# Two passes of a transformer layer with experts: the key pass without TensorE transposes, and another order of work on ScalarE and VectorE in the expert pass

## Chip, cores and metric

The kernel runs on one core of a Trainium2 chip. The metric is the device time of one execution, in microseconds (us). Three runs of the kernel before took 6706.5, 6708.36 and 6711.54 us; the median is 6708.36 us.

## What is computed

`T` = 4096 tokens (4 batches of 1024) with `H` = 1024 features. In float32:

```python
def _layernorm(x): m, v = mean(x), var(x); return (x - m) / sqrt(v + 1e-5)
# cross attention, 16 heads of 64
q = layernorm(x) @ Wq.T + bq;  k = ctx @ Wk.T + bk;  v = ctx @ Wv.T + bv
probs = softmax(clip(where(mask, q @ k.T / 8, -1e4), -50, 50))
delta = (probs @ v) @ Wo.T + bo
x = x + layernorm(rs * delta) * gamma + beta
# experts: 64, each token goes to 8, I = 384
h = layernorm(x)
scores = softmax(h @ gate_weight.T); topk_w, topk_idx = top_k(scores, 8); topk_w /= sum(topk_w)
x = x + sum over the 8 of topk_w * ((silu(h @ w_gate[e]) * (h @ w_up[e])) @ w_down[e])
```

Every large product is made of three matrix products: each operand is split into a rounded part (`hi`, a cast on ScalarE) and the rest (`lo`, a subtraction on VectorE), and `hi*hi + hi*lo + lo*hi` is accumulated.

## The kernel before

The program is a chain of passes with a barrier between them: projections (keys K, values V, queries Q), attention, output with routing, and experts. All waits are written out by hand as semaphore waits, so each engine works through its own list in the order of the program text.

**Projections** (`projections_pass`). Three products K, V, Q, one after the other, each over 8 blocks of 512 tokens. A block has 8 rounds `g`, each of 24 matmuls of 512 columns (L420 to L422) into one of 4 PSUM banks; ScalarE and VectorE evacuate them (L293, L355), SyncE stores. Activations come by GpSimd's DMA queue into `a_raw` (L192) in 4 pieces, are split by `high` (L282) and `low` (L342) in rounds 0 to 3 of the block before, and are double-buffered as `a_hi`, `a_lo`. In the key pass VectorE also normalizes the 32 tiles of 128 tokens of `x` (`layernorm`, ending in `xn`, L373), one in every second round. TensorE turns each in 8 transposes of 128x128 (L431) into PSUM, ScalarE copies it out (`transposed`, L304), and SyncE stores it by features into the scratch `xnT` (L264), from which the query pass loads its activations.

**Experts** (`experts_pass`). Work goes by tiles of 128 routed tokens: 286 tiles in this run, for 64 experts, each with `n` tiles (read from `dir_sb`). `tile t` means, engine by engine in list order:

- TensorE: gate (24 matmuls of 384 columns, L1374 to L1376), up (24 more), then down of tile t-1 (18 matmuls of 512 columns, L1361 to L1363), then 3 transposes of `hidden` (L1381). At the first tile of an expert it waits piece by piece for that expert's split weights.
- ScalarE: `silu` of tile t (L1432), `xT_hi` of tile t+1 (L1408), `y` of tile t-1 from PSUM (L1414), `hT_hi` (L1438). In an expert's first tile the 8 pieces (128x768) of the next expert's gate and up weights are cast (L1402) between `xT_hi` and `y`, and the loads of the gate and up weights after those are issued at the end (`load_gate_up`, L1420; it waits until VectorE has done all 8 pieces). After the last tile of an expert come the 3 pieces of the next down weights (L1402), and then their next load (`load_down`, L1426; it waits for VectorE's 3 pieces). Then the numbers of the next expert are read from `dir_sb` into registers (L1250, L1251).
- VectorE: `hidden` = silu * weight * up (L1484), `xT_lo` of tile t+1 (L1471), the turn of the gathered tokens of tile t+2 in 32x32 blocks (L1477), in a first tile the 8 pieces of `gu_lo` (L1467), then `hT_lo` (L1491), and at the end of an expert the 3 pieces of `d_lo`.
- GpSimd: for tile t+3 it waits for the turn of t+2, makes the row numbers (L1321, 128x4 integers from the records in `rec_g`), waits for them, and issues 4 gathers (L1325); then it issues the scatter of `y` of tile t-1, which adds to `out` in DRAM (L1335).
- SyncE: small loads of records (L1262, L1277). The records of tile t+4 are loaded after the row numbers of tile t+3 are made.

`y` has one buffer, so the copy of `y` waits until the scatter before it has landed:

```python
def output(t, is_first=False):
    act.wait_ge(down_done, t + 2)
    if not is_first:
        act.wait_ge(added, 16 * (t + 1))
    nc.scalar.copy(y[:], y_ps[:]).then_inc(y_done, 1)
```

## Time and profile before

| what | value |
|---|---|
| median of 3 runs | 6708.36 us (6706.5 to 6711.54) |
| profiled execution, its time | 6714.65 us |
| its span | 6713.0 us |
| TensorE busy, matmuls / weight loads | 6472.6 us (96%) / 5731.1 us (85%) |
| VectorE, ScalarE, GpSimd busy | 3663.3, 2923.7, 2308.0 us |
| mean granted TensorE clock | 0.983 |
| first matmul of the expert pass | at 2852.5 us |
| GB/s moved over the span | 156 |

All times inside the kernel are those of the profiled execution, counted from its first instruction. A matmul's duration in the rows is longer than its share of TensorE's time, because matmuls overlap: in a run of them the distance between starts counts (0.23 us for 512 columns, 0.17 us for 384).

### The profile page before, as it was taken

The page shows a single profiled execution, that of the slowest core. Times are in us where ns is not written, and L with a number is a line of the kernel's source. Part 1 is how long each engine was busy: PE and PEld are TensorE (multiplying, and loading weights), DVE is VectorE, ACT ScalarE, POOL GpSimd, SP SyncE. Part 2 cuts the span into 40 slices and gives each one's busy share as a digit, 9 for nine tenths or more (in the row PEclk, how much of TensorE's full clock was granted, in tenths as well). Part 3 has the DMA queues.
Part 4 walks back from the last instruction along what each step waited for, and adds up shares of the span by engine and source line. Part 5 has one row for each costly group of instructions (what it writes and reads, how often), then busy time and mean ns, then how long its engine had stood idle before and what let it go on. Part 6 is the DMA issues. An engine that isn't in the chain of part 4 may idle for free.

```text
span 6713.0 us, 107844 instructions
## 1 busy us (share of the span) xinstructions
PE 6472.6 (96%) x32234; PEld 5731.1 (85%) x32235; DVE 3663.3 (55%) x4544; ACT 2923.7 (44%) x3606; POOL 2308.0 (34%) x2178
## 2 busy tenths in 40 slices
PE   9999999999999999699999999999999999999998
PEld 7888887887888788589989888899899999989987
DVE  4443324999999799744454454443533444444444
ACT  3321224888888655333343343332422333333333
POOL 1000000000000155544545454554444444545554
PEclk9999999999999999899999999999999999999999
DMA  8863555555555676456676676665655656666666
GB/s 258 232 196 143 155 146 144 127 128 127 128 132 130 174 173 171 110 152 160 163 212 162 164 188 160 163 164 111 186 111 111 139 137 164 146 155 164 161 158 149
DMA packets 873577, 1049.72 MB, mean 156 GB/s; under 512 B 440705, under 2 KB 670849, under 8 KB 873474
## 3 DMA queue, kind: packets, MB, share of 16 engines
q0 software_dynamic: 123984, 368.70, 24.0%
q1 hardware_dynamic: 593104, 382.50, 23.6%
q10 hardware_dynamic: 156386, 297.29, 13.2%
q8 instruction: 48, 0.79, 0.1%
q14 instruction: 55, 0.45, 0.0%
HBM read 725.85 MB, written 322.31 MB: 156 GB/s over the span
## 4 chain that ended last, share of the span: by engine, by line
PE 33%; DMA 8%; issue 6%; DVE 4%; POOL 3%; ACT 2%; ACTq 1%; SPq 0%; another core or an unknown queue 0%; POOLq 0%; DVEq 0%
DMA out<-moe_y,moe_rec_s 4%; PE moe_ps_gate L1374 4%; PE moe_ps_gate L1375 4%; PE moe_ps_gate L1376 4%; PE moe_ps_up L1376 4%; PE moe_ps_up L1374 4%; PE moe_ps_up L1375 4%; PE moe_ps_y L1363 3%; PE moe_ps_y L1362 3%; PE moe_ps_y L1361 3%; DMA moe_tokens<-h2st,moe_rows 3%; POOL moe_tokens L1325 2%; DVE moe_ps_turned L1477 1%; DVE moe_d_lo L1467 1%; DVE moe_gu_lo L1467 1%
## 5 line engine op out<-in xcount | busy, mean ns | idle before, releaser
L1325 POOL DMA_INDIRECT moe_tokens<-h2st,moe_rows x1156 | 1273.1, 1101 | 515.2 <-issue 265.7
L1374 PE MATMUL moe_ps_gate<-moe_gu_hi,moe_xT_hi 128*128 128x384 f32 x2288 | 811.3, 355 | 73.8 <-DVE moe_xT_lo L1471 53.9
L1414 ACT COPY moe_y<-moe_ps_y 128x1024 f32<-128x1024 f32 x287 | 291.2, 1015 | 1249.4 <-DMA out<-moe_y,moe_rec_s 1051.9
L1375 PE MATMUL moe_ps_gate<-moe_gu_lo,moe_xT_hi 128*128 128x384 f32 x2288 | 784.4, 343 | 0.0
L1376 PE MATMUL moe_ps_gate<-moe_gu_hi,moe_xT_lo 128*128 128x384 f32 x2288 | 783.4, 342 | 0.0
L1376 PE MATMUL moe_ps_up<-moe_gu_hi,moe_xT_lo 128*128 128x384 f32 x2288 | 764.3, 334 | 0.0
L1375 PE MATMUL moe_ps_up<-moe_gu_lo,moe_xT_hi 128*128 128x384 f32 x2288 | 764.2, 334 | 0.0
L1374 PE MATMUL moe_ps_up<-moe_gu_hi,moe_xT_hi 128*128 128x384 f32 x2288 | 764.2, 334 | 0.0
L1484 DVE SCALAR_TENSOR_TENSOR moe_hidden<-moe_silu,moe_rec_w,moe_ps_up 128x384 f32<-128x384 f32 x286 | 175.8, 615 | 1009.2 <-PE moe_ps_up L1376 694.4
L1361 PE MATMUL moe_ps_y<-moe_d_hi,moe_hT_hi 128*128 128x512 f32 x1722 | 673.5, 391 | 12.8 <-DVE moe_hT_lo L1491 10.3
L1363 PE MATMUL moe_ps_y<-moe_d_hi,moe_hT_lo 128*128 128x512 f32 x1722 | 677.1, 393 | 0.0
L1362 PE MATMUL moe_ps_y<-moe_d_lo,moe_hT_hi 128*128 128x512 f32 x1722 | 675.7, 392 | 0.0
L657 DVE TENSOR_TENSOR att_p_lo<-att_p,att_p_hi 128x1024 fp32r<-128x1024 f32 x512 | 626.5, 1224 | 58.9 <-ACT att_p_hi L626 53.2
L626 ACT CAST att_p_hi<-att_p 128x1024 fp32r<-128x1024 f32 x512 | 539.7, 1054 | 161.5 <-PE att_ps_o L597 158.0
L1321 POOL TENSOR_SCALAR moe_rows<-moe_rec_g,moe_group 128x4 int32<-128x4 int32 x289 | 156.6, 542 | 1245.5 <-DVE moe_ps_turned L1477 1190.1
L1491 DVE TENSOR_TENSOR moe_hT_lo<-moe_ps_hT,moe_hT_hi 128x384 fp32r<-128x384 f32 x286 | 158.8, 555 | 736.6 <-ACT moe_hT_hi L1438 646.3
L1335 POOL DMA_INDIRECT out<-moe_y,moe_rec_s x287 | 491.1, 1711 | 185.5 <-issue 177.1
L620 ACT ACTIVATE att_e<-att_ps_sc 128x1024 f32<-128x1024 f32 x512 | 522.5, 1021 | 10.3 <-PE att_ps_sc L583 10.3
L1477 DVE STREAM_TRANSPOSE moe_ps_turned<-moe_tokens 128x1024 f32<-128x1024 f32 x288 | 362.9, 1260 | 292.7 <-DMA moe_tokens<-h2st,moe_rows 272.7
L1374 PEld LDWEIGHTS moe_ps_gate<-moe_gu_hi,moe_xT_hi 128*128 128x128 f32 x2288 | 444.4, 194 | 86.1 <-issue 47.3
L1408 ACT CAST moe_xT_hi<-moe_ps_turned 128x1024 fp32r<-128x1024 f32 x287 | 290.8, 1013 | 511.1 <-PE moe_ps_up L1376 442.5
L1467 DVE TENSOR_TENSOR moe_gu_lo<-first_raw,moe_gu_hi 128x768 fp32r<-128x768 f32 x512 | 448.3, 943 | 0.4 <-ACT moe_gu_hi L1402 0.3
(202 smaller groups left out, 14047.6 us busy)
## 6 DMA issues: line engine op xcount, KB each, us to landing
first_raw<-in_w_gate ACTq DMA_DIRECT2D x63, 1536.0 KB, 7.7
first_raw<-in_w_up ACTq DMA_DIRECT2D x63, 1536.0 KB
moe_raw_d<-in_w_down ACTq DMA_DIRECT2D x63, 1536.0 KB
proj_a_raw<-in_ctxT POOLq DMA_DIRECT2D x64, 512.0 KB, 5.6
kst<-proj_o SPq DMA_DIRECT2D x256, 128.0 KB, 2.8
vst<-proj_o SPq DMA_DIRECT2D x64, 512.0 KB, 2.6
qst<-proj_o SPq DMA_DIRECT2D x256, 128.0 KB, 2.2
att_kt<-kst SPq DMA_DIRECT2D x64, 512.0 KB, 3.5
```

Of the source, the lines that this page charges most:

```text
L620: nc.scalar.activation(e32[:, u % 2], sc[:, u % 2], ACT.Exp, scale=1.0 / math.sqrt(HD)).then_inc(exp_done, 1)
L626: nc.scalar.copy(p_hi[:, u % 2], p32[:, u % 2]).then_inc(hi_done, 1)
L657: nc.vector.tensor_tensor(p_lo[:, u % 2], p32[:, u % 2], f32(p_hi[:, u % 2]), ALU.subtract).then_inc(lo_done, 1)
L1325: nc.gpsimd.indirect_dma_start(out=tokens[:, g * (H // G):(g + 1) * (H // G)], out_offset=None, in_=h2_quarters, in_offset=bass.IndirectOf ...
L1335: nc.gpsimd.indirect_dma_start(out=acc[:, :], out_offset=bass.IndirectOffsetOnAxis(ap=rec_s[:].bitcast(I32)[:, 0:1], axis=0), in_=y[:], in ...
L1361: nc.tensor.matmul(y_ps[:, cols], hT_hi[:, c], d_hi[:, b, c, cols], start=(c == 0), stop=False)
L1362: nc.tensor.matmul(y_ps[:, cols], hT_hi[:, c], d_lo[:, b, c, cols], start=False, stop=False)
L1363: last = nc.tensor.matmul(y_ps[:, cols], hT_lo[:, c], d_hi[:, b, c, cols], start=False, stop=(c == CI - 1))
L1374: nc.tensor.matmul(o[:, 0:I], xT_hi[:, c], gu_hi[:, b, k, c], start=(c == 0), stop=False)
L1375: nc.tensor.matmul(o[:, 0:I], xT_hi[:, c], gu_lo[:, b, k, c], start=False, stop=False)
L1376: last = nc.tensor.matmul(o[:, 0:I], xT_lo[:, c], gu_hi[:, b, k, c], start=False, stop=(c == C - 1))
L1467: nc.vector.tensor_tensor(low, raw, f32(high), ALU.subtract).then_inc(w_lo_done, 1)
```

## The change

Projections: the normalized tiles are stored as rows (`xnst`, tokens by features), with the columns of each row permuted by quarters in the write of `xn`. TensorE's 256 transposes, ScalarE's 32 copies and the PSUM tile are gone. In the query pass GpSimd's queue loads 512 token rows at a time (4 loads of 512 KB, each into 32 partitions) into `xg`, which takes the place of `xin` and `xn`, and VectorE turns them in 32x32 blocks, 4 turns of 128x1024 for each of the 8 query blocks, in rounds 0 to 3 of the block before, ahead of that round's evacuation. `high` and `low` read `a_raw` through a permuted view.

Experts: `silu` of tile t+1 is issued at the end of tile t, ahead of what follows a tile (weight pieces of the down product, register loads). Gate and up weights are split in 4 pieces of 128x1536 in place of 8 of 128x768, and they stand between other work. The three weight loads are issued at other places. Row numbers are made by VectorE. Scatter and gathers keep their order.

```diff
@@ projections, SyncE, then VectorE, then TensorE @@
+                            sp.dma_start(xnst[bass.ds(j * P, P), :], xn[:, jb]).then_inc(xn_stored[jb], 16)
...
+                def turn(p, t2, b, k):
+                    n = number(p, t2, b)
+                    dve.wait_ge(xg_in, 16 * (P // W) * (2 * t2 + b + 1))
+                    dve.wait_ge(a_lo_done, (n - 1) * PIECES + k + 1)
+                    columns_of_piece = slice(k * CP * W, (k + 1) * CP * W)
+                    nc.vector.transpose(a_raw[:, chunks(k)].rearrange("p c t -> p (c t)"), xg[:, :, columns_of_piece]).then_inc(turned_done, 1)
...
-                        dve.wait_ge(t_done, j - 1)
-                    nc.vector.tensor_scalar(xn[:, jb], xin[:, jb], mv[:, jb, 0:1], rstd[:, jb],
+                        dve.wait_ge(xn_stored[jb], 16 * (LN // 2 * (2 * t2 + b) + g // 4))
+                    nc.vector.tensor_scalar(by_quarter(xn[:, jb]), in_chunks(xin[:, jb]), mv[:, jb, 0:1], rstd[:, jb],
...
-                            for c in range(C):
-                                last = nc.tensor.transpose(tps[:, jb, c], xn[:, jb, c * P:(c + 1) * P], ident[:])
-                            last.then_inc(t_done, 1)
@@ experts, pieces and GpSimd @@
+        CHUNKS = C // 2
+        GU = 2 * C // CHUNKS
+        PIECES = GU + CI
...
                 def gather(t):
-                    pool.wait_ge(rec_g_in, 16 * G * (t + 1))
                     pool.wait_ge(turned_done, t)
                     pool.sem_inc(pool_passed, 1)
-                    nc.gpsimd.tensor_scalar(rows[:], rec_g[:].bitcast(I32)[:, :, 0], float(G), group[:], ALU.mult, ALU.add).then_inc(rows_done, 1)
                     pool.wait_ge(rows_done, t + 1)
@@ experts, end of TensorE's list @@
+                pe.wait_ge(hidden_done, last_tile + 2)
+                pe.sem_inc(gu_done, 1)
                 down(last_tile, (E - 1) % 2)
@@ experts, ScalarE @@
+                def load_gate_up(e, k):
+
+                    act.wait_ge(w_lo_done, PIECES * (e - 1) + (k + 1) * GU // 2)
...
+                def tile(t):
+                    tokens_high(t + 1)
+                    output(t - 1)
+                    turned_high(t)
+                    gated(t + 1)
+
+                def first_tile(t, e, b, more, is_first):
+                    tokens_high(t + 1)
+                    load_down(e)
+                    split(e, b, 0, 2)
+                    output(t - 1, is_first)
+                    split(e, b, 2, 3)
+                    turned_high(t)
+                    split(e, b, 3, GU)
+                    gated(t + 1)
                     if more:
-                        load_gate_up(e + 1)
+                        load_gate_up(e + 1, 0)
+                        load_gate_up(e + 1, 1)
...
                         split(e + 1, 1 - b, GU, PIECES)
-                        if has_second:
-                            load_down(e + 2)
@@ experts, VectorE @@
+                def token_rows(t):
+                    dve.wait_ge(rec_g_in, 16 * G * (t + 1))
+                    if not (isinstance(t, int) and t == 0):
+                        dve.wait_ge(gathered, 16 * G * t)
+                    nc.vector.tensor_scalar(rows[:], rec_g[:].bitcast(I32)[:, :, 0], float(G), group[:], ALU.mult, ALU.add).then_inc(rows_done, 1)
...
                     tokens_low(t + 1)
+                    if e is not None:
+                        split(e, b, 0, 1)
                     turn_tokens(t + 2)
+                    token_rows(t + 3)
                     if e is not None:
-                        split(e, b, 0, GU)
+                        split(e, b, 1, 2)
+                    if e is not None:
+                        split(e, b, 2, 3)
                     dve.wait_ge(hT_hi_done, t + 1)
                     nc.vector.tensor_tensor(hT_lo[:], hT_ps, f32(hT_hi[:]), ALU.subtract).then_inc(hT_lo_done, 1)
+                    if e is not None:
+                        split(e, b, 3, GU)
```

Here `gated(t)` is the `silu` of tile t with its two waits, `turned_high(t)` is `hT_hi`, and `tokens_high(t + 1)` is `xT_hi`.

## Rows read from the trace of the kernel before

**Rows 1.** The page, busy time of each engine over the span.
```profile
PE 6472.6 (96%) x32234; PEld 5731.1 (85%) x32235; DVE 3663.3 (55%) x4544; ACT 2923.7 (44%) x3606; POOL 2308.0 (34%) x2178
```
**Rows 2.** Groups by line, TensorE, first 1100 us: count | busy, mean ns | idle before.
```profile
L431 PE MATMUL proj_ps_tps<-proj_ident,proj_xn 128*128 128x128 f32 x256 | 33.1, 272 | 0.0
```
**Rows 3.** Timeline, TensorE, around one group of transposes: start us, us.
```profile
48.93 1.03 PE L431 MATMUL proj_ps_tps<-proj_ident,proj_xn 128*128 128x128 f32 x8
49.72 0.48 PE L420 MATMUL proj_ps_acc<-proj_a_hi,proj_w_hi 128*128 128x512 f32 x1
```
**Rows 4.** DMA issues by line: count, KB each, median us from issue to landing.
```profile
proj_a_raw<-xnT POOLq DMA_DIRECT2D x32, 512.0 KB, 4.4
```
**Rows 5.** TensorE's waits, 2853 us to the end: total us, times, longest.
```profile
PE moe_ps_hT L1381 <- DVE moe_hidden L1484: 61.4, 26, 3.2
PE moe_ps_gate L1374 <- DVE moe_xT_lo L1471: 53.9, 27, 37.8
```
**Rows 6.** View by tile of `hidden`: ns min/median/max, first and last start.
```profile
L1484 DVE SCALAR_TENSOR_TENSOR moe_hidden<-moe_silu,moe_rec_w,moe_ps_up x286: 612/615/618, 2865.7 to 6685.1; 128x384 f32<-128x384 f32 x143
```
**Rows 7.** Timeline, ScalarE, an expert's two tiles and the next expert's start.
```profile
4752.38 1.01 ACT L1408 CAST moe_xT_hi<-moe_ps_turned 128x1024 fp32r<-128x1024 f32 x1 [0.26 <-PE moe_ps_up L1376]
4753.29 5.98 ACT L1402 CAST moe_gu_hi<-first_raw 128x768 fp32r<-128x768 f32 x8
...
4765.50 0.49 ACT L1432 ACTIVATE moe_silu<-moe_ps_gate 128x384 f32<-128x384 f32 x1 [4.42 <-issue]
...
4775.48 1.02 ACT L1414 COPY moe_y<-moe_ps_y 128x1024 f32<-128x1024 f32 x1 [8.58 <-DMA out<-moe_y,moe_rec_s]
...
4776.76 2.95 ACT L1402 CAST moe_d_hi<-moe_raw_d 128x1024 fp32r<-128x1024 f32 x3
4781.51 0.39 ACTq L1426 DMA_DIRECT2D moe_raw_d<-in_w_down  x1
4783.65 0.49 ACT L1432 ACTIVATE moe_silu<-moe_ps_gate 128x384 f32<-128x384 f32 x1 [3.94 <-issue]
```
**Rows 8.** Timeline, VectorE, the same stretch and the tile before it.
```profile
4739.66 0.61 DVE L1484 SCALAR_TENSOR_TENSOR moe_hidden<-moe_silu,moe_rec_w,moe_ps_up 128x384 f32<-128x384 f32 x1 [6.72 <-PE moe_ps_up L1376]
...
4752.47 0.61 DVE L1484 SCALAR_TENSOR_TENSOR moe_hidden<-moe_silu,moe_rec_w,moe_ps_up 128x384 f32<-128x384 f32 x1 [2.83 <-PE moe_ps_up L1376]
...
4771.73 1.26 DVE L1477 STREAM_TRANSPOSE moe_ps_turned<-moe_tokens 128x1024 f32<-128x1024 f32 x1 [3.57 <-DMA moe_tokens<-h2st,moe_rows]
...
4784.43 0.61 DVE L1484 SCALAR_TENSOR_TENSOR moe_hidden<-moe_silu,moe_rec_w,moe_ps_up 128x384 f32<-128x384 f32 x1 [3.08 <-ACT moe_silu L1432]
```
**Rows 9.** Timeline, GpSimd, the same stretch.
```profile
4743.43 0.27 POOL L1321 TENSOR_SCALAR moe_rows<-moe_rec_g,moe_group 128x4 int32<-128x4 int32 x1 [4.98 <-DVE moe_ps_turned L1477]
...
4745.86 0.95 POOL L1325 DMA_INDIRECT moe_tokens<-h2st,moe_rows  x1 [0.30 <-issue]
...
4757.19 1.54 POOL L1321 TENSOR_SCALAR moe_rows<-moe_rec_g,moe_group 128x4 int32<-128x4 int32 x1 [4.80 <-DVE moe_ps_turned L1477]
4759.57 1.74 POOL L1325 DMA_INDIRECT moe_tokens<-h2st,moe_rows  x1 [0.84 <-POOL moe_rows L1321]
...
4766.26 1.63 POOL L1335 DMA_INDIRECT out<-moe_y,moe_rec_s  x1 [0.30 <-issue]
```
**Rows 10.** Timeline, TensorE, the transposes and the gate product after them.
```profile
4785.10 0.55 PE L1381 MATMUL moe_ps_hT<-moe_ident,moe_hidden 128*128 128x128 f32 x3 [2.95 <-DVE moe_hidden L1484]
...
4786.84 0.52 PE L1375 MATMUL moe_ps_gate<-moe_gu_lo,moe_xT_hi 128*128 128x384 f32 x1
4787.16 0.52 PE L1376 MATMUL moe_ps_gate<-moe_gu_hi,moe_xT_lo 128*128 128x384 f32 x1
```
**Rows 11.** Groups by line and shape, ScalarE and VectorE, 2853 us to the end.
```profile
L1402 ACT CAST moe_gu_hi<-first_raw 128x768 fp32r<-128x768 f32 x506 | 378.7, 838 | 12.3 <-DMA first_raw<-in_w_up 11.4 <-DMA first_raw<-in_w_gate 0.8
L1467 DVE TENSOR_TENSOR moe_gu_lo<-first_raw,moe_gu_hi 128x768 fp32r<-128x768 f32 x508 | 444.8, 943 | 0.4 <-ACT moe_gu_hi L1402 0.3
L1467 DVE TENSOR_TENSOR moe_d_lo<-moe_raw_d,moe_d_hi 128x1024 fp32r<-128x1024 f32 x192 | 223.8, 1221 | 34.6 <-ACT moe_d_hi L1402 25.2 <-issue 9.4
```

More of the change, by code:

```diff
@@ L146, in stores_before @@
         def stores_before(p, t2, b, g):
-            return 16 * (sum(STORES[i] * NB * G // 2 for i in range(p)) + STORES[p] * ((2 * t2 + b) * (G // 2) + g // 2))
+            return 16 * (sum(STORES[i] * NB * ROUNDS // 2 for i in range(p)) + STORES[p] * ((2 * t2 + b) * (ROUNDS // 2) + g // 2))
         def piece(p, half, k):
@@ L163, in norm_tile, with turned, split @@
             return LN * (2 * t2 + b) + g // 2 if g % 2 == 0 else None
-        def transposed_tile(p, t2, b, g):
-            if g % 2 == 0 or p == Q or p == V and not (is_first(t2, b) and g == 1) or p == K and is_first(t2, b) and g == 1:
-                return None
-            if p == V:
-                return LN * NB - 1
-            return LN * (2 * t2 + b) + (g - 3) // 2
-        def stored_tiles(p, t2, b, g):
-            return LN // 2 * (NB if p == V else 2 * t2 + b) + (g - 3) // 2 // 2
+        def turned(p, k):
+            raw = a_raw[:, chunks(k)]
+            if p < Q:
+                return raw
+            return raw.rearrange("p c t -> p (c t)").rearrange("p (g c b) -> p c g b", g=GROUPS, b=W)
+        def split(p, tile, b, k):
+            piece = tile[:, b, chunks(k)]
+            if p < Q:
+                return piece
+            return piece.rearrange("p c (g b) -> p c g b", b=W)
         def chunks(k):
@@ L188, in load @@
                     n, t = number(p, t2, b), 2 * t2 + b
+                    if p == Q:
+                        if not is_first(t2, b):
+                            pool.wait_ge(turned_done, PIECES * t)
+                        for k in range(P // W):
+                            part = xnst[bass.ds(t * HALF, HALF), k * (H * W // P):(k + 1) * (H * W // P)]
+                            pool.dma_start(xg[k * W:(k + 1) * W], part.rearrange("(g b) n -> b g n", b=W)).then_inc(xg_in, 16)
+                        return
                     for k in range(PIECES):
@@ L280, in high @@
                     n = number(p, t2, b)
[L281 to L282 removed]
+                    if p < Q:
+                        act.wait_ge(a_in[k], 16 * (n + 1))
+                    else:
+                        act.wait_ge(turned_done, (2 * t2 + b) * PIECES + k + 1)
+                    nc.scalar.copy(split(p, a_hi, b, k), turned(p, k)).then_inc(a_hi_done, 1)
                 def evacuate(p, t2, b, g):
[L285 removed]
+                    n, q = number(p, t2, b) * ROUNDS + g, g % 2
                     if not (p == K and is_first(t2, b) and g < 2):
@@ L298, in root @@
                     nc.scalar.activation(std[:, jb], mv[:, jb, 1:2], ACT.Sqrt, bias=eps[:]).then_inc(std_done, 1)
-                def transposed(j, jb, tiles_before):
-                    act.wait_ge(t_done, j + 1)
-                    if not (known(tiles_before) and tiles_before == 0):
-                        act.wait_ge(xT_stored[jb], 16 * tiles_before)
-                    nc.scalar.copy(xT[:, jb], tps[:, jb]).then_inc(xT_done, 1)
                 for k in range(PIECES):
@@ L316, in body @@
                         weights_high(p, 1, 1)
-                    for g in range(G):
+                    for g in range(ROUNDS):
                         evacuate(p, t2, b, g)
@@ L386, in body @@
                         weights_low(p, 1, 1)
-                    for g in range(G):
+                    for g in range(ROUNDS):
+                        if after and after[0] == Q and g < PIECES:
+                            turn(*after, g)
                         evacuate(p, t2, b, g)
@@ L1371, in tile @@
                         for c in range(C):
-                            if e is not None and c % 2 == 0:
-                                pe.wait_ge(w_lo_done, PIECES * e + k * (C // 2) + c // 2 + 1)
+                            if e is not None and c % CHUNKS == 0:
+                                pe.wait_ge(w_lo_done, PIECES * e + (k * C + c) // CHUNKS + 1)
                             nc.tensor.matmul(o[:, 0:I], xT_hi[:, c], gu_hi[:, b, k, c], start=(c == 0), stop=False)
@@ L1426, in load_down, with gated @@
                     act.dma_start(raw_d[:], w_down[bass.ds(e, 1)].rearrange("o (c p) i -> p (o c) i", p=P)).then_inc(raw_in[2], 16)
-                def tile(t, e=None, b=None, more=False, is_first=False):
+                def gated(t):
                     act.wait_ge(gu_done, 2 * t + 1)
```

119 lines of the change are left out of this document (49 added, 70 removed).

## The prediction

> **What bounds the kernel now.** I read the busy times first. TensorE is busy 96% of the span [rows 1], so little can be won but by taking work off TensorE or by closing its gaps. The change touches two passes, and I ask of each which of the two it does.
>
> In the key pass the groups by line show TensorE's transposes, 256 of them, with no idle time before them [rows 2]. The timeline shows what they take: a group of 8 starts at 48.93 and the next product at 49.72, so 0.79 us of TensorE's own queue, in a pass that otherwise never waits [rows 3]. There are 32 such groups.
>
> In the expert pass I took the distance between `hidden` instructions as the length of a tile. Undisturbed it is 4752.47 - 4739.66 = 12.81 us [rows 8], and that is TensorE's own: 48 x 0.173 + 18 x 0.228 + 0.3. The whole pass took 6685.1 - 2865.7 = 3819.4 us for 285 distances [rows 6], against 285 x 12.80 = 3648. So 171 us are lost, and only they can be won. TensorE's waits say where: 61.4 us in 26 waits for `hidden`, and some 16 us in 26 waits for `xT_lo` (53.9 less the one of 37.8 at the pass's start) [rows 5]. After such a wait the gate product runs with starts 4787.16 - 4786.84 = 0.32 us apart [rows 10], where 0.17 is usual: the granted clock is at its lower level (1.2 GHz) there, after TensorE stood still for 2.95 us. About 12 matmuls run so, 1.8 us more. A stall thus costs 2.4 + 0.6 + 1.8 = 4.8 us, and 26 of them make 124 of the 171.
>
> All 26 are at an expert's first tile. Counted in the trace, the loss there is 7.3 us behind an expert of one tile (6 cases), 5.1 behind two (11), 5.2 behind three (10), 1.1 behind four (10) and 0.1 behind longer ones (25). The timelines show one case, behind two tiles; times are from 4752.4, when up of the first tile ended. ScalarE casts eight pieces. GpSimd's row numbers take 1.54 us where they take 0.27 elsewhere, and a gather 1.74 where it takes 0.95 [rows 9], so the scatter is issued only at +13.9 (4766.26). It lands about +22.8, and `y` starts at +23.1 [rows 7]. Then `hT_hi`, three pieces to +27.3, the load at +29.1 (which waits for VectorE's pieces), register reads, and only at +31.3 `silu` [rows 7], so `hidden` at +32.0 [rows 8]. TensorE wanted it at 25.6 + 4.1 = +29.7 and waited 2.95 us [rows 10].
>
> **The change, part by part.**
> *Transposes off TensorE*: 32 x 0.79 = 25.3 us, all on the path. What comes in their place lies beside TensorE. VectorE gets 32 turns of 1.26 us, the duration of the turn in the expert pass [rows 8]; that one writes PSUM and this one SBUF, so I bound it by 1.2 and 2.5 us. It stands in rounds of 24 x 0.227 = 5.4 us, beside an evacuation and a split of some 2 us, and TensorE is four banks away from noticing. The permuted write of `xn` can at most double a 0.8 us instruction in every second round of the key pass, with as much room. If that cover were gone, 32 x 1.26 = 40 us would show. The new loads have 32 partitions as target; loads of this size landed in 4.4 us [rows 4]. They have about half a block, 20 us, so even four times as long costs nothing; I take 0.
> *`silu` at the end of ScalarE's list*: inside a run of tiles the order is the same. At the end of an expert `silu` no longer stands behind three pieces, a load with its wait and register reads, 31.3 - 24.4 = 6.9 us in the case shown. Late next is `xT_hi`, which is now behind pieces and register reads. It may start 2.0 us after up has ended (1.0 for it, 0.1, 1.2 for `xT_lo`, before the gate product at +4.4).
> *Four wide pieces*: VectorE's durations rise from 943 to 1221 ns for 256 columns more [rows 11], so 1536 columns take 1.78; 4 x 1.78 = 7.1 against 8 x 0.94 = 7.5. ScalarE's I put at 1.5 (under 2 x 0.84). The sum is hardly less, but three pieces in place of eight stand ahead of `hT_lo`.
> *Row numbers by VectorE*: from turn to first gather GpSimd now needs 0.3 + 0.27 + 0.84 us in a plain tile and 2.7 in a first tile [rows 9]. VectorE's version is not in the trace; I bound it by 0 and 0.27 us and take 0.15, and the wake-up of GpSimd by 0.3 (its gap between gathers) and 0.84, and take 0.6. That gives 0.7 us in plain tiles; in first tiles the turn itself is behind a piece. The new wait for `rec_g` holds up VectorE's pieces and `hT_lo`, which TensorE needs at the tile's end, 3 us later than it comes. 0.
> *Loads*: the down load moves from an expert's end (a tile before, or late in a short expert) to +0.5 of the next first tile; the gate load is issued at about +9, the up load at +11.5, where both were at +12. The scatter meets as much traffic as now. TensorE's and ScalarE's last extra steps lie under the last down product. 0.
>
> The same case worked through anew: turn at +4.3, gathers +6.3 to +12.7, scatter +13.0, landed +22.1 (8.9 after its issue, as now, 13.9 to 22.8). Then `y` to +23.1, `hT_hi` to +23.6, `silu` to +24.1, so `hidden` is on time. Pieces to +27.2, register reads 1.0 (between 0, if they overlap the last piece, and the 2.1 from load to `silu` [rows 7]) to +28.2, which is 2.6 after up's end at +25.6 where 2.0 is allowed: 0.6 us lost. `hT_lo` of that tile loses another 0.9. So behind two tiles 1.5 is left of 5.1, 11 x 3.6 = 40 won. Behind three or four tiles pieces and registers end in time: 10 x 5.2 + 10 x 1.1 = 63 won. Behind one tile everything of two experts meets, weight loads included: I leave 5 of 7.3, 6 x 2.3 = 14 won. At the start of the pass, VectorE's `hT_lo` is 3 us sooner. Together 120, of which I keep 110 for mis-sized gaps.
>
> Sum: 25 + 110 = 135 us off 6714.65, the profiled execution's own time, which stands 6.3 above the median of the runs. From the median: 6708.4 - 135 = 6573.
>
> **Rivals.**
> (a) *Half of the stalls stay.* Down, gate and up loads now follow one another from +0.5 on, 4.5 MB in one stretch beside the gathers, and a turn already waited 3.57 us for gathers beside a load [rows 8]. If gathers or scatter take 2 us longer in first tiles, `hT_lo` of the next tile comes after +25.6. For it: the margin is about 1 us. Against it: each load has the traffic that it has now. 25 + 55 = 80 us, so 6628.
> (b) *Only the key pass pays.* Experts as before: 6683. It needs stalls in long experts too to eat the gain.
> (c) *Slower: GpSimd is held behind the wide pieces.* The rows show GpSimd's steps drawn out just while VectorE subtracts weights, 0.27 to 1.54 and 0.95 to 1.74 [rows 9], so about one narrow piece of 0.94 us at a time. If each of four gathers waits for a wide piece, it takes 1.78 + 0.30 (the gap) at the least and 0.95 more at the most, and they end at +14.6 to +18.4 against +12.7. The point from which it decides is +14.5: then scatter (0.3), landing and `y` (9.2), copy and `hT_hi` (1.6) end at +25.6, and TensorE waits for `hT_lo` in every one of 63 experts. At the middle, +16.5, that is 2.0 us and 1.8 of clock, 63 x 3.8 = 239 us, less the 135: 6708 + 104 = 6812. Against it: VectorE has only 5.3 us of wide pieces behind the turn, as against 7.0 now, and gaps between them. The Trainium skill, page "SBUF — State Buffer", section "SBUF: two separate sides", says that VectorE, with two SBUF inputs, and GpSimd take their shared port for a whole instruction, and the other blocks; by that rule the wide piece is the worse one, and (c) would come true if the gathers' descriptors are always caught by it.
> (d) *The change doesn't do what it says.* If the turns on VectorE take so long that the evacuations fall behind four rounds, 25 us are lost again: with (b), 6708.
>
> **How the numbers follow.** Forecast 0.60, (a) 0.18, (b) 0.11, (d) or nothing gained 0.04, (c) 0.07. Within 0.2% is 13.4 us, about what a measurement of this kernel can tell from no change. Faster: 0.60 + 0.18 + 0.11 = 0.89; same 0.04; slower 0.07. The forecast's own bounds are 6530 (all of the first tiles' loss gone, 171 - 15 = 156 and 25) and 6610. Taking in (a) up to 6660 brings about 0.78; so 6530 to 6660.
>
> **What would show it.** No transposes in the key pass and the attention pass starting 25 us sooner; TensorE's waits for `hidden` under 10 us, for `xT_lo` and `hT_lo` 10 to 30; `hidden` distances of 12.8 behind experts of three tiles or more; first gather under 1 us behind the row numbers. It is wrong if first tiles show TensorE waiting for `hT_lo` or for `gu_lo` by more than 1 us each, or if gathers in first tiles get longer than 1.74 us.

## The result, and the profile after

The changed kernel takes 6653.4 us (median of 4 runs, 6648.3 to 6660.2) where the kernel before takes 6709.4 on the same chip: ratio 0.9917, 95% interval 0.9901 to 0.9933. The forecast was 6573 us. So 56 us are won of 135; the time lies inside the range, and the size is wrong by more than half. The profiled execution took 6652.08 us, with a span of 6650.5. Below, every ratio is to the kernel before, timed on the same chip beside the kernel named; an interval is some 0.0017 to either side, 11 us, so a difference between ratios from two chips is good to some 16 us. One of the four executions of the kernel with the wait moved took 11930 us at a granted clock of 0.81 and is left out of its ratio.

The page's busy times, answering to [rows 1]:

```profile
PE 6427.3 (97%) x31978; PEld 5677.5 (85%) x31979; DVE 3705.8 (56%) x4609; ACT 2871.8 (43%) x3319; POOL 2112.3 (32%) x1887
```

TensorE has 256 instructions fewer. Where the time came from is read off the stages' first products (the first instruction of each pass on TensorE). The attention pass:

```profile
1104.72 0.77 PE L582 MATMUL att_ps_sc<-att_qh,att_kt 128*128 128x512 f32 x1 [15.69 <-DMA att_ql<-qst]
```

```profile
1076.53 0.77 PE L578 MATMUL att_ps_sc<-att_qh,att_kt 128*128 128x512 f32 x1 [16.05 <-DMA att_ql<-qst]
```

The first line is of the kernel before, the second of the changed one: 28.2 us sooner. The expert pass starts 29.6 us sooner (2852.5 to 2822.9). The rest of the 62.5 us between the two spans is the expert pass. Its `hidden`, answering to [rows 6]:

```profile
L1502 DVE SCALAR_TENSOR_TENSOR moe_hidden<-moe_silu,moe_rec_w,moe_ps_up x286: 600/614/617, 2834.8 to 6622.8; 128x384 f32<-128x384 f32 x143
```

6622.8 - 2834.8 = 3788.0 for the same 285 distances, against 3819.4. Of the 171 us lost before, 140 are still lost, and the forecast had 110 won. TensorE's waits, 2822 us to the end, answering to [rows 5]:

```profile
PE moe_ps_gate L1371 <- DVE moe_xT_lo L1483: 46.2, 24, 36.9
PE moe_ps_y L1358 <- DVE moe_hT_lo L1514: 44.5, 34, 4.5
PE moe_ps_y L1358 <- issue: 14.4, 24, 1.8
PE moe_ps_gate L1371 <- DVE moe_gu_lo L1479: 12.1, 10, 2.6
PE moe_ps_hT L1378 <- DVE moe_hidden L1502: 8.9, 9, 1.6
```

The waits for `hidden` are gone (61.4 to 8.9). In their place stand 34 waits for `hT_lo`, 44.5 us, and 24 more at the same product, 14.4 us, for which the trace names no releaser; the mean granted clock rose from 0.983 to 0.988. Counted by tile (the distance between transposes less 12.8), the loss in first tiles fell from 94 to 38 us, in second tiles it stayed (75 to 71), and in third tiles it rose from 3 to 32.

A calm first tile (no tile before it late; up ends at 3761.8) shows why. ScalarE:

```profile
3754.05 0.48 ACT L1434 CAST moe_hT_hi<-moe_ps_hT 128x384 fp32r<-128x384 f32 x1
3757.84 0.49 ACT L1430 ACTIVATE moe_silu<-moe_ps_gate 128x384 f32<-128x384 f32 x1 [3.30 <-PE moe_ps_gate L1373]
3758.22 2.94 ACT L1401 CAST moe_d_hi<-moe_raw_d 128x1024 fp32r<-128x1024 f32 x3
3761.74 1.02 ACT L1407 CAST moe_xT_hi<-moe_ps_turned 128x1024 fp32r<-128x1024 f32 x1 [0.58 <-PE moe_ps_up L1373]
```

VectorE:

```profile
3759.29 3.50 DVE L1479 TENSOR_TENSOR moe_d_lo<-moe_raw_d,moe_d_hi 128x1024 fp32r<-128x1024 f32 x3 [4.17 <-ACT moe_d_hi L1401]
3764.24 0.61 DVE L1502 SCALAR_TENSOR_TENSOR moe_hidden<-moe_silu,moe_rec_w,moe_ps_up 128x384 f32<-128x384 f32 x1 [1.45 <-issue]
...
3765.91 1.75 DVE L1479 TENSOR_TENSOR moe_gu_lo<-first_raw,moe_gu_hi 128x1536 fp32r<-128x1536 f32 x1
3767.57 1.25 DVE L1495 STREAM_TRANSPOSE moe_ps_turned<-moe_tokens 128x1024 f32<-128x1024 f32 x1
3768.73 0.19 DVE L1489 TENSOR_SCALAR moe_rows<-moe_rec_g,moe_group 128x4 int32<-128x4 int32 x1
...
3787.30 0.56 DVE L1514 TENSOR_TENSOR moe_hT_lo<-moe_ps_hT,moe_hT_hi 128x384 fp32r<-128x384 f32 x1 [4.62 <-ACT moe_hT_hi L1434]
```

GpSimd:

```profile
3769.80 1.64 POOL L1322 DMA_INDIRECT moe_tokens<-h2st,moe_rows  x1 [9.56 <-DVE moe_rows L1489]
3771.75 1.33 POOL L1322 DMA_INDIRECT moe_tokens<-h2st,moe_rows  x1 [0.30 <-issue]
3773.38 1.82 POOL L1322 DMA_INDIRECT moe_tokens<-h2st,moe_rows  x1 [0.30 <-issue]
...
3776.76 1.63 POOL L1332 DMA_INDIRECT out<-moe_y,moe_rec_s  x1 [0.30 <-issue]
```

ScalarE was done with `hT_hi` at 3754.5. Then `silu` waits 3.30 us for the gate product of the next expert, and the three down pieces, which were ready to be cast, stand behind it. VectorE's three follow at 3759.29, its register reads after them, and `hidden` comes 2.4 us after up's end, the turn at +5.8 (forecast +4.3), the scatter at +15.0 (+13.0), and `hT_lo` of the next tile at +25.5. It takes 0.56 us and is done at +26.1. TensorE could have gone on at +25.5 (its last matmul of up started at 3787.13, and they come 0.17 apart), so it waits:

```profile
3787.91 0.50 PE L1358 MATMUL moe_ps_y<-moe_d_hi,moe_hT_hi 128*128 128x512 f32 x1 [0.44 <-DVE moe_hT_lo L1514]
```

### The profile page after: what moved, and what is told of

It is laid out like the page before. It is cut to its first block, busy times and chain, and to the rows that moved or that the text cites. A ratio compares the mean times of both kernels' runs of the same rounds, so it can differ in the third digit from the quotient of the medians.

```text
span 6650.5 us, 106922 instructions
## 1 busy us (share of the span) xinstructions
PE 6427.3 (97%) x31978; PEld 5677.5 (85%) x31979; DVE 3705.8 (56%) x4609; ACT 2871.8 (43%) x3319; POOL 2112.3 (32%) x1887
## 3 DMA queue, kind: packets, MB, share of 16 engines
q0 software_dynamic: 123984, 368.70, 24.8%
## 4 chain that ended last, share of the span: by engine, by line
PE 32%; DMA 9%; issue 8%; POOL 3%; DVE 2%; SPq 1%; ACT 1%; DVEq 1%; another core or an unknown queue 0%; ACTq 0%; POOLq 0%
DMA out<-moe_y,moe_rec_s 6%; PE moe_ps_gate L1373 4%; PE moe_ps_y L1358 4%; PE moe_ps_gate L1371 4%; PE moe_ps_gate L1372 3%; PE moe_ps_y L1360 3%; PE moe_ps_y L1359 3%; PE moe_ps_up L1373 3%; PE moe_ps_up L1371 3%; PE moe_ps_up L1372 3%; POOL moe_tokens L1322 3%; DMA moe_rec_g<-table 1%; DMA moe_tokens<-h2st,moe_rows 1%; PE moe_ps_hT L1378 1%; DVE moe_d_lo L1479 1%
## 5 line engine op out<-in xcount | busy, mean ns | idle before, releaser
L1322 POOL DMA_INDIRECT moe_tokens<-h2st,moe_rows x1156 | 1243.9, 1076 | 1875.1 <-DVE moe_rows L1489 1604.5
L1371 PE MATMUL moe_ps_gate<-moe_gu_hi,moe_xT_hi 128*128 128x384 f32 x2288 | 795.4, 348 | 58.4 <-DVE moe_xT_lo L1483 46.2
L1372 PE MATMUL moe_ps_gate<-moe_gu_lo,moe_xT_hi 128*128 128x384 f32 x2288 | 770.7, 337 | 0.0
L1373 PE MATMUL moe_ps_gate<-moe_gu_hi,moe_xT_lo 128*128 128x384 f32 x2288 | 769.4, 336 | 0.0
L1358 PE MATMUL moe_ps_y<-moe_d_hi,moe_hT_hi 128*128 128x512 f32 x1722 | 684.3, 397 | 59.1 <-DVE moe_hT_lo L1514 44.5
L1479 DVE TENSOR_TENSOR moe_gu_lo<-first_raw,moe_gu_hi 128x1536 fp32r<-128x1536 f32 x256 | 444.7, 1751 | 56.7 <-ACT moe_gu_hi L1401 52.5
L1358 PEld LDWEIGHTS moe_ps_y<-moe_d_hi,moe_hT_hi 128*128 128x128 f32 x1722 | 327.8, 190 | 140.5 <-DVE moe_hT_lo L1514 55.6
```

The lines of the kernel that those rows point to most:

```text
L1322: nc.gpsimd.indirect_dma_start(out=tokens[:, g * (H // G):(g + 1) * (H // G)], out_offset=None, in_=h2_quarters, in_offset=bass.IndirectOf ...
L1358: nc.tensor.matmul(y_ps[:, cols], hT_hi[:, c], d_hi[:, b, c, cols], start=(c == 0), stop=False)
L1371: nc.tensor.matmul(o[:, 0:I], xT_hi[:, c], gu_hi[:, b, k, c], start=(c == 0), stop=False)
L1372: nc.tensor.matmul(o[:, 0:I], xT_hi[:, c], gu_lo[:, b, k, c], start=False, stop=False)
L1373: last = nc.tensor.matmul(o[:, 0:I], xT_lo[:, c], gu_hi[:, b, k, c], start=False, stop=(c == C - 1))
L1479: nc.vector.tensor_tensor(low, raw, f32(high), ALU.subtract).then_inc(w_lo_done, 1)
```

## The experiments

Fourteen kernels. Theory 1: VectorE's down pieces make `hidden` and the turn late. Theory 2: SyncE loads the token records too late, since it waits for the scatter first (VectorE's row numbers wait 133.6 us for them in 42 waits). Theory 3: wide pieces hold GpSimd. Theory 4 came out of the first eight runs and stands below.

**Only the projections changed.** The expert pass is the one of before.

> Only the projections are the changed ones; the expert pass is the one of before. The stage starts of the changed kernel (attention 28.2 us sooner, first gate product 29.6 us sooner) say that this part alone is worth 28 to 30 us: 6709 - 29 = 6680, ratio 0.9957, and the expert pass then shows the waits of before: some 61 us for `hidden`. If the new projections disturb nothing behind them, the expert pass is as long as before (3819 us from first to last `hidden`). If the ratio is under 0.993, the expert part of the change is worth less than the 31 us that the two traces give it; over 0.999, more.

Ratio 0.9952 (0.9936 to 0.9969), 32 us; TensorE waits 56.7 us for `hidden`. So the key pass gives what the stage starts said, and the expert part of the change gives 0.9952 - 0.9917 = 0.35%, some 24 us (31 by the two traces).

**VectorE's down pieces moved** into the first tile, ScalarE's left where they are (theory 1).

```diff
                     turn_tokens(t + 2)
                     token_rows(t + 3)
+                    if own is not None:
+                        split(*own, GU, PIECES)
...
-                        split(e + 1, 1 - b, GU, PIECES)
```

> The changed kernel, but VectorE's three pieces of the down weights stand in the expert's first tile behind turn and row numbers instead of at the end of the expert before, and the down load is issued two pieces later. Theory 1 (the turn of a first tile comes late because these pieces and VectorE's register reads now stand ahead of `hidden`: 2.4 us behind up's end instead of 0.5): the turn starts at about +3.6 instead of +5.8, gathers end at +12.5 instead of +14.7, TensorE's waits for `hT_lo` fall from 44.5 us to under 15, and the time falls by 20 to 40 us, to 6615 to 6635. Theory 2 (the row numbers are late because SyncE loads the token records only after the scatter has landed): VectorE's waits for the records stay at some 130 us in all, blocks with a late scatter stay, and the gain is under 10 us. Theory 3 (GpSimd is held behind wide pieces): the gathers start sooner and fall among just as many pieces, three more in fact, so they take longer and the time stays at 6653 or rises.

Ratio 1.0405 (1.0388 to 1.0422): far slower than any theory said, for a reason that none of them had. TensorE's waits:

```profile
PE moe_ps_gate L1371 <- DVE moe_d_lo L1479: 294.0, 58, 8.9
```

TensorE's wait for the down pieces stands right behind the first tile's transposes, not where the product needs them. This run says nothing of the theories; the run with the wait moved (below) does.

**Records loaded first** (theory 2).

```diff
                     record(rec_w, t + 1, rec_w_in)
+                    sp.wait_ge(rows_done, t + 4)
+                    sp.sem_inc(sp_passed, 1)
+                    record_groups(record_rows(t + 4))
                     if not is_first:
                         sp.wait_ge(added, 16 * t)
```

> The changed kernel, but SyncE issues the token records of tile t+4 as soon as the row numbers of t+3 are made, ahead of its wait for the scatter. Theory 2 (late records): VectorE's waits for the records fall from 133.6 us to under 20, the distances of 18 to 20 us between transposes go, TensorE's waits for `hT_lo` fall by a third or more, and the time falls by 10 to 20 us, to 6633 to 6643. Theory 1 (late `hidden` and turn in first tiles): the waits for the records vanish too, but the turn of a first tile stays at +5.8 and `hT_lo` at the limit, so the gain is 5 us or less. Theory 3 (wide pieces hold GpSimd): no difference.

Ratio 0.9957 (0.9941 to 0.9974), 27 us slower than the changed kernel's ratio, against every theory. The waits for the token records went, but the scatter's own record now comes late. GpSimd's waits:

```profile
POOL out L1332 <- DMA moe_rec_s<-table: 207.3, 67, 6.2
```

This was 36.9 us in 13 waits in the changed kernel. SyncE stands still for the row numbers while the scatter before has landed: a wait was exchanged for another that lies on the path.

**Narrow pieces**, eight of 128x768 at the same four places (theory 3): `CHUNKS = C // 4`, and the indices in `split` doubled.

> The changed kernel with gate and up weights split in 8 pieces of 128x768 at the same four places, in place of 4 of 128x1536. Theory 3 (wide pieces hold GpSimd): the gathers of a first tile come 1 us or more closer together (they took 1.64, 1.33, 1.82 and 0.95 us with wide pieces), end before +13.7, and the time falls by 10 us or more. Theories 1 and 2: the pieces' sum rises by 0.4 us for VectorE and 0.6 us for ScalarE in each first tile (8 x 0.94 against 4 x 1.75), `hT_lo` comes that much later, and the time is the same to 10 us more: 6653 to 6663.

Ratio 0.9898 (0.9881 to 0.9914), 13 us less than the changed kernel's ratio, but the intervals overlap. Behind experts of three or more tiles the gathers of a first tile take 6.0 us in place of 6.7 (medians). A pair of kernels on one chip, with two more edits in both, settles it below.

**Down pieces later, wait moved**: as two runs before, but TensorE waits ahead of the expert's first down product, and the down load is issued behind `hT_hi`.

> As the run with the down pieces moved into the expert's first tile, but TensorE waits for them where it needs them, ahead of the first down product of that expert (a tile later), and the down load stands behind `hT_hi`. In the run before this one the wait stood right behind the first tile's transposes, at +4.4, and cost 294 us in 58 waits. Theory 1 (`hidden` and turn of the first tile late by VectorE's pieces and register reads): with the wait out of the way the turn starts at +3.6 to +4.5 behind up's end, gathers end by +13.5, waits for `hT_lo` and `d_lo` together are under 15 us, and the time is 20 to 40 us below the changed kernel's ratio of 0.9917, that is 0.986 to 0.989. Rival (the gathers' own loop, landing then turn then row numbers then gathers, sets the length in first tiles wherever the turn stands): the ratio is 0.990 to 0.993.

Ratio 0.9929 (0.9909 to 0.9949), as the rival said, though not for its reason. `hidden` is on time and the turn starts at +3.0 (median), but the pieces only moved: `hT_lo` of the first tile now comes at +12.7, and TensorE waits for weights instead.

```profile
PE moe_ps_y L1358 <- DVE moe_gu_lo L1480: 54.5, 43, 5.3
...
PE moe_ps_gate L1371 <- DVE moe_gu_lo L1480: 29.4, 6, 5.5
```

**Turn first**: turn and row numbers ahead of VectorE's first gate piece.

```diff
-                    if e is not None:
-                        split(e, b, 0, 1)
                     turn_tokens(t + 2)
                     token_rows(t + 3)
                     if e is not None:
-                        split(e, b, 1, 2)
+                        split(e, b, 0, 2)
```

> The changed kernel with turn and row numbers of a first tile ahead of VectorE's first gate piece instead of behind it. The turn can start 1.75 us sooner, at +4.0 instead of +5.8, if its tokens are there. Theory 1: gathers end at about +13, the 44.5 us of waits for `hT_lo` fall to under 20, and the ratio is 0.987 to 0.989. Rival (the pieces that TensorE's next gate product needs are what is late, or the gathers' landing is): the turn waits for the tokens, `hT_lo` waits stay over 35 us and the ratio stays 0.990 to 0.993.

Ratio 0.9868 (0.9849 to 0.9886); the waits for `hT_lo` fall to 27.3 us in 14. The late turn is worth some 33 us of the changed kernel (0.9917 - 0.9868), clear of the intervals.

**Row numbers on GpSimd** again.

> The changed kernel with the row numbers made by GpSimd again, as before the change. If VectorE's wait for the records (133.6 us in 42 waits) matters, undoing it gains or is even: ratio 0.989 to 0.992, `hT_lo` waits under 44.5 us. If the quicker way from turn to first gather (0.34 us sooner in plain tiles, 1 to 2 us in first tiles) is what counts, undoing it costs 10 to 25 us: ratio 0.993 to 0.996, and the first gather of a first tile starts over 2 us behind the turn's end.

Ratio 1.0047 (1.0030 to 1.0063): slower even than the kernel before, by far more than either theory said. The calm first tile, GpSimd and then VectorE:

```profile
3800.31 3.14 POOL L1320 TENSOR_SCALAR moe_rows<-moe_rec_g,moe_group 128x4 int32<-128x4 int32 x1 [8.38 <-DVE moe_ps_turned L1492]
3804.30 2.14 POOL L1324 DMA_INDIRECT moe_tokens<-h2st,moe_rows  x1 [0.85 <-POOL moe_rows L1320]
```

```profile
3800.00 3.39 DVE L1482 TENSOR_TENSOR moe_gu_lo<-first_raw,moe_gu_hi 128x1536 fp32r<-128x1536 f32 x2
```

An instruction that takes 0.27 us alone [rows 9] ends at 3803.45, as VectorE's two wide pieces do (3803.39). The first gather of a calm first tile starts at +11.0 (median), where it was +7.9 in the changed kernel. The Trainium skill, page "SBUF — State Buffer", section "SBUF: two separate sides", says that a VectorE operation with two SBUF inputs and a GpSimd operation that reads SBUF share a pair of ports: the one that starts first has it for its whole instruction, and the other is blocked. The trace agrees that GpSimd does not end before VectorE does, and shows that this held across two pieces in a row.

**`silu` at the head of ScalarE's list** again, all else changed.

```diff
                 def tile(t):
+                    gated(t)
                     tokens_high(t + 1)
                     output(t - 1)
                     turned_high(t)
-                    gated(t + 1)
```

> The changed kernel with `silu` at the head of ScalarE's list again (behind down pieces, loads and register reads), all else changed. If the place of `silu` is what removed TensorE's waits for `hidden` (61.4 us in 26 before, 8.9 in 9 after), they come back to over 40 us and the ratio rises to 0.995 or more. If the shorter distance to `y` and the pieces at other places removed them, they stay under 20 us and the ratio stays 0.990 to 0.993.

Ratio 0.9893 (0.9876 to 0.9909), and TensorE's waits for `hidden` are 2.5 us. So the step on which the forecast rested was not needed to remove them: undone, they are still gone, and the kernel is no slower. It is hardly faster either (16 us, the intervals overlap), and its trace loses as much of the pass as the changed kernel's, 140.5 us against 140.0:

```profile
PE moe_ps_y L1358 <- DVE moe_hT_lo L1513: 48.1, 27, 4.4
```

ScalarE in the calm first tile (up ends at 3767.5):

```profile
3759.66 0.49 ACT L1434 CAST moe_hT_hi<-moe_ps_hT 128x384 fp32r<-128x384 f32 x1
3760.03 2.96 ACT L1401 CAST moe_d_hi<-moe_raw_d 128x1024 fp32r<-128x1024 f32 x3
3764.31 0.49 ACT L1430 ACTIVATE moe_silu<-moe_ps_gate 128x384 f32<-128x384 f32 x1 [1.32 <-PE moe_ps_gate L1373]
```

The down pieces now run right behind `hT_hi`, 3.9 us sooner against up's end (-7.5 where it was -3.6), and `silu` is as early as it need be. That is theory 4: `silu`'s wait for the next gate product is what makes `hidden` and the turn of a calm first tile late. In calm tiles it holds. That the kernel loses as much all the same is made up elsewhere: summed over a first tile and the two behind it (means), `silu` at the head loses 0.1 us in place of 1.1 behind experts of five or more tiles and 4.1 in place of 4.8 behind three, but 6.1 in place of 3.9 behind two and 7.9 in place of 6.8 behind one. What it loses more there is open.

**Both edits**, `silu` at the head and turn first.

> The changed kernel with two edits together: `silu` at the head of ScalarE's list, so that the down pieces do not stand behind its wait for the next gate product, and turn and row numbers of a first tile ahead of all gate pieces. Theory 4 (what delays the turn of a first tile is `silu`, whose wait for the next expert's gate product holds up ScalarE's three down pieces, and with them VectorE's, its register reads and `hidden`; then a gate piece ahead of the turn): `hidden` of calm first tiles is on time (distance 12.8), the turn starts at +2.3 to +3, gathers end at about +11.3, TensorE's waits for `hT_lo` fall under 20 us, and the ratio is 0.981 to 0.985, under each of the two edits alone (0.9893 and 0.9868). Rival (both edits win the same microseconds, or the loss left comes from one-tile experts and late records): 0.986 to 0.989.

Ratio 0.9803 (0.9786 to 0.9819), 6568.0 us, below what was expected, and more than the two edits give apart (0.24% and 0.49% against the changed kernel, 1.14% or some 77 us together). TensorE's waits:

```profile
PE moe_ps_y L1358 <- DVE moe_hT_lo L1511: 19.0, 13, 4.6
...
PE moe_ps_hT L1378 <- DVE moe_hidden L1501: 0.5, 2, 0.3
```

Only 59 us of the pass are still lost. VectorE's waits for the token records:

```profile
DVE moe_rows L1488 <- DMA moe_rec_g<-table: 0.3, 1, 0.3
```

133.6 us of them went with no edit to the records. They went with the late tiles, so they were a consequence and not a cause, and theory 2 falls.

**The same with narrow pieces**, on the same chip.

> The run with both edits, but 8 narrow pieces in place of 4 wide ones at the same places. If a gather is held until VectorE's piece has ended (the four gathers of a first tile took 6.7 us with wide pieces and 6.0 with narrow ones, 4.8 without pieces), narrow pieces win up to 0.7 us a first tile and the ratio is 0.002 to 0.004 lower than with wide ones; if the longer sum of the pieces outweighs it, it is the same within 0.001 or 0.001 to 0.003 higher.

Ratio 0.9791 (0.9775 to 0.9807). The two kernels' runs do not overlap (6558.7 to 6561.3 against 6566.0 to 6570.4): narrow pieces win 8 us. The gathers of a first tile end at +11.0 instead of +11.6 (medians). Theory 3 is right in kind and small, as long as the row numbers are VectorE's.

**Changed projections and row numbers on VectorE alone**, the rest of the expert pass as before.

> Changed projections, and the expert pass of before with only the row numbers made by VectorE. The projections alone gave 0.9952. Making the row numbers on GpSimd again in the changed kernel cost 1.3%. If that is the worth of the row numbers by themselves, this kernel reaches 0.985 or less. If the 1.3% was the price of row numbers on GpSimd among wide pieces (3.1 us for one of them, until two wide pieces had ended, where it was 1.5 among narrow ones), the gain here is smaller, 0.2 to 0.5%: 0.990 to 0.993. If it is nothing, 0.995.

Ratio 0.9943 (0.9926 to 0.9959), against 0.9952 for the projections alone: the row numbers by themselves are worth 0.1%, less than the intervals can tell from nothing. Among narrow pieces GpSimd can make them as well; among wide ones that costs 1.3% (the run above).

**The scatter's record loaded by ScalarE**, added to both edits, so that SyncE never waits for the scatter.

```diff
                 def output(t, is_first=False):
+                    row = act.value_load(dir_sb[0:1, bass.ds(row_at + 1 + t, 1)], min_val=0, max_val=table.shape[0] - P)
                     if not is_first:
                         act.wait_ge(added, 16 * (t + 1))
+                    act.sem_inc(act_passed, 1)
+                    act.dma_start(rec_s[:], table[bass.ds(row, P), :]).then_inc(rec_s_in, 16)
+                    act.wait_ge(down_done, t + 2)
```

> The run with both edits, and ScalarE's queue loads the record of the scatter right behind its own wait for the scatter before, so that SyncE has only the other records to load and never waits for the scatter. Theory 2 in its second form (late token records): VectorE's waits for them fall from some 130 us to under 30, nothing else moves, and the ratio falls by 0.001 to 0.004 against the run with both edits. Rival (the records are late only where the tile is late anyway, so what waits is not on the path; or ScalarE's extra register read costs as much): within 0.001, or higher.

Ratio 0.9825 (0.9809 to 0.9842), 15 us slower than both edits on the same chip, as the rival said: next to nothing waited for the token records in that kernel (0.3 us). TensorE's waits for `hidden` rose from 0.5 to 6.0 us and for `hT_lo` from 19.0 to 23.8; that this is ScalarE's longer list ahead of `y` was not tried by itself.

**The down load back at the expert's end**, in the best kernel.

```diff
                         split(e + 1, 1 - b, GU, PIECES)
+                        if has_second:
+                            load_down(e + 2)
```

> The best kernel so far (`silu` at the head of the list, turn first, narrow pieces: ratio 0.9791, TensorE's waits for `hidden` 0.8 us), with the down load back at an expert's end, behind its down pieces and with its wait for VectorE's. If it was this load, with its wait on ScalarE ahead of `silu`, that made `hidden` late in the kernel before (61.4 us in 26 waits), the waits for `hidden` come back to over 30 us and the ratio rises by 0.005 or more. If it was the pieces in one block ahead of `y`, they stay under 10 us and the ratio stays within 0.002 of 0.9791.

Ratio 0.9942 (0.9926 to 0.9959): 101 us lost by one load's place. TensorE's waits, then ScalarE around a first tile whose up product ends at 3766.5:

```profile
PE moe_ps_hT L1378 <- DVE moe_hidden L1503: 55.5, 23, 4.0
```

```profile
3759.14 2.96 ACT L1401 CAST moe_d_hi<-moe_raw_d 128x1024 fp32r<-128x1024 f32 x3
3763.91 0.38 ACTq L1425 DMA_DIRECT2D moe_raw_d<-in_w_down  x1
3765.95 0.49 ACT L1430 ACTIVATE moe_silu<-moe_ps_gate 128x384 f32<-128x384 f32 x1 [3.84 <-issue]
```

The load waits for VectorE's last down piece (until 3763.8), the register reads come after it, and `silu` starts 3.7 us later than in a plain tile (4.2 ahead of up's end, 3762.3).

**All pieces in one block**, the other difference left to the kernel before.

> The same kernel with the down load where the change put it, but the eight pieces in one block again: ahead of `y` on ScalarE, ahead of `hT_lo` on VectorE. If the block is what made `hidden` late in the kernel before (its scatter, `y`, `hT_hi` and down pieces come one after another, and `y` could not start before the eighth cast at +6.5), the waits for `hidden` come back to over 30 us and the ratio rises by 0.005 or more; `hT_lo` of the first tile starts at about +11 instead of +8.7. If it was the down load, they stay under 10 us and the ratio within 0.002 of 0.9791.

Ratio 0.9789 (0.9773 to 0.9805), 6559.7 us on the chip where the down load at the end took 6660.9. Spreading the pieces over the tile is worth nothing that can be measured.

**First tiles side by side.** The medians over the 45 first tiles behind an expert of three or more tiles, start of each instruction in us from up's end (the transposes' start less 3.83, their distance in a plain tile):

| | before | changed | `silu` at head | both edits | narrow, down load at end |
|---|---|---|---|---|---|
| last down cast | -5.2 | -1.7 | -5.5 | -5.5 | -5.5 |
| `silu` | -0.5 | -3.9 | -3.1 | -4.2 | -0.6 |
| `hidden` | 0.3 | 2.2 | 0.0 | 0.0 | 0.2 |
| turn | 3.6 | 5.7 | 4.0 | 2.3 | 3.2 |
| first gather | 7.4 | 7.9 | 6.2 | 4.5 | 5.4 |
| `hT_lo` of the next tile | 24.7 | 25.6 | 23.9 | 22.9 | 24.8 |

In the last row the changed kernel is 0.9 us worse than the kernel before, and that is over the limit: `hT_lo`, which takes 0.56 us, ends only after TensorE is through with the up product of the tile in 36 of the 45 cases. In the kernel before it does so in 8, with `silu` at the head in 6, with both edits in 3, and with the down load at the end in 15.

## Why the prediction was right, and where it was wrong

*Transposes off TensorE*: right. 25.3 us were forecast; 28.2 show at the attention pass, and 32 in the run of this part alone. Where the 3 us above the transposes come from was not tried. The turns took 1.24 us (forecast 1.26), and TensorE waited for none of them.

***`silu` at the end of ScalarE's list*, with a wide piece ahead of the turn: this is the step that failed.** The 110 us of the expert pass were measured as 31 (171 lost before, 140 after). The prediction said of `silu` that `silu` "no longer stands behind three pieces, a load with its wait and register reads", and "Late next is `xT_hi`, which is now behind pieces and register reads". Nothing behind `silu` was priced beyond that. But `silu` waits for the next gate product, so at a calm expert's end it holds up three down casts by 3.8 us. The way on runs over VectorE: its down pieces, its register reads, `hidden` at +2.2, the turn, the gathers, the scatter, and `hT_lo` a tile later, 0.4 us too late at the median. The worked case (behind two tiles) has `silu` at +24.1, when the gate product had long ended, so the wait didn't show in it. Nor did `hidden` come on time in the eleven cases of that kind: `silu` starts 0.6 us before up's end, but `hidden` at +4.6 (median), right behind VectorE's own down pieces, which end at +4.3 and of which the prediction says nothing there. From this one case followed "Behind three or four tiles pieces and registers end in time: 10 x 5.2 + 10 x 1.1 = 63 won". For their first tiles that came true (0 lost), and the second and third tiles lost it again. What the place of `silu` costs depends on the turn: 16 us in the changed kernel, within the intervals, and 44 us with the turn first (0.9868 against 0.9803).

The second half of the step is the gate piece that VectorE got ahead of the turn. It was listed ("in first tiles the turn itself is behind a piece") and is in the turn's +4.3 of the worked case, but no loss was put to it. It costs 33 us in the changed kernel (0.9917 - 0.9868) and 60 with `silu` at the head (0.9893 - 0.9803). Both halves together are 1.14%, 77 us, nearly all of the 110 - 31 = 79 us that the pass fell short.

*Loads*: "0" was wrong, by the largest amount of all. The move of the down load is what took away the waits for `hidden`. The prediction saw this load ahead of `silu` in [rows 7] (at +29.1, `silu` at +31.3), and credited `silu`'s new place with it. With the load moved, the waits stay away wherever `silu` stands (8.9 us with it at the end, 2.5 at the head); the edit credited with removing them was not needed, and is the one that costs. No run has `silu` at the end and the load at its old place, so whether `silu`'s new place would have been enough too is not shown. In the best kernel the load's place is worth 101 us.

*Wide pieces*: 1.75 and 1.48 us against 1.78 and 1.5 forecast. That three in place of eight stand ahead of `hT_lo` won nothing (one block 0.9789, spread 0.9791), and wide ones cost 8 us.

*Row numbers by VectorE*: the way from row numbers to first gather was 1.07 us between starts, 0.88 from end to start, within the "under 1 us" given. The new wait for the records, put at 0, shows as 133.6 us on VectorE, but goes by itself once the tiles are on time (0.3 us); what it costs in the changed kernel no run tells alone. What the row numbers on VectorE are worth depends on the pieces: 0.1%, within the intervals, among narrow ones, 1.3% among wide ones.

*The rivals.* (a) is nearest, 6628 against 6653: its place was right (`hT_lo` after +25.6), its cause is not shown, since no run has the loads' traffic as what makes the gathers late. (c)'s point, gathers ending after +14.5, was reached at the median of calm first tiles (14.6), though not by its mechanism: the gathers took 6.7 us from first to last, near the 6.4 of the forecast, and began 1.6 late. Its mechanism is real where GpSimd makes the row numbers, and took that kernel above the time before. (b) and (d) did not come.

*What would show it*: TensorE's waits for `hidden` under 10 us (8.9) and the sooner attention pass came true. Distances of 12.8 between `hidden` instructions behind experts of three or more tiles did not (15.0 into the first tile, median), nor did waits for `hT_lo` of 10 to 30 us (44.5). Two of the rows named as signs of being wrong are there: `hT_lo` late, and a gather of 1.82 us in a first tile, over the 1.74.

The forecast's 6573 us rested on a first tile with `hidden` on time, the turn at +4.3 and the gathers done at +12.7. The kernel with `silu` at the head alone has just that at the median (0.0, 4.0 and 13.0), takes 6643 us, and still loses 140 us of the pass, nearly all of it behind experts of one to four tiles. The kernel with both edits takes 6568, with the turn two microseconds sooner than the forecast had it. So that one tile timed right did not give the time of the pass, and that 6568 lies near 6573 is luck.

## What to carry to other kernels

When an instruction with a wait is moved on an in-order engine, write down what now stands behind it and follow each of those to the other engines, in the calm case as well as in the late one: an instruction put early to be early holds up the rest until its own wait ends. When two edits of a change aim at the same stall, undo each by itself before crediting either. A tile that comes out as worked does not price the pass: count the loss over all tiles, by the length of what stands ahead of them. A wait that grows beside a loss need not be its cause: remove the lateness first and look whether it goes too.

## What the runs showed of the hardware

A GpSimd instruction of 0.27 us took 3.14 beside VectorE's two pieces of 128x1536 and ended with the second. From the first gather's start to the last one's end it took 4.8 us in plain tiles, 6.0 in first tiles of the changed kernel with narrow pieces, and 6.7 with wide ones (medians, behind experts of three or more tiles).

In the kernel with the down pieces moved, ScalarE's `silu` started up to 6.3 us after the instruction before it, in 74 waits, 1.7 to 3.2 us after the gate product had ended, and the trace names no releaser:

```profile
3729.17 0.49 ACT L1430 ACTIVATE moe_silu<-moe_ps_gate 128x384 f32<-128x384 f32 x1 [6.26 <-remote]
```

The gate product's last matmul had started at 3725.58. What holds `silu` there stays open; in the changed kernel it is 13 such waits, 56 us together, each 1.7 us after the gate product's end.
